# Self attention: where TensorE weighs a batch within a step

## What is computed

```python
def _L1_attn_ref(x, Wqkv, Wout, Wpos, coeffs):
    ...
    pos_bias = jnp.einsum('ijf,hf->hij', pos_feat, Wpos)
    qkv = jnp.einsum('bsd,ed->bse', x, Wqkv)
    q, k, v = jnp.split(qkv, 3, axis=-1)
    ...
    logits = jnp.einsum('bihd,bjhd->bhij', q, k) * scale + pos_bias[None]
    attn = jax.nn.softmax(logits, axis=-1)
    out = jnp.einsum('bhij,bjhd->bihd', attn, v).reshape(B, S, D)
    return jnp.einsum('bsd,ed->bse', out, Wout)
...
    x = x + _L1_attn_ref(_layernorm(x, axis=-1), L1_attn_Wqkv, L1_attn_Wout, L1_attn_Wpos, L1_attn_coeffs)
```

## Time and profile before

| | |
|---|---|
| time, three runs | 1470.67, 1470.76, 1476.12 us; median 1470.76 |
| span of the profiled execution | 1470.8 us; the page gives no other time for it |
| busy, TensorE / VectorE / ScalarE / GpSimd | 94% / 62% / 54% / 45% of the span |
| mean granted clock of TensorE | 0.984 of full speed |
| the stage of the change | about 714 to 956 us |

### The profile page before, as it was taken

How to read it: one execution, slowest core, us unless ns; L and a number is a source line. 1 busy time by engine, 2 the same in 40 slices (tenths; PEclk the granted TensorE clock), 3 DMA queues, 4 the chain that set the end, 5 groups by cost and what they waited for, 6 DMA issues and landing times.

```text
span 1470.8 us, 38209 instructions
## 1 busy us (share of the span) xinstructions
PE 1379.5 (94%) x14581; PEld 1051.8 (72%) x14581; DVE 917.2 (62%) x2370; ACT 796.8 (54%) x1526; POOL 655.2 (45%) x680
## 2 busy tenths in 40 slices
PE   6999999997999989999789998899999999998997
PEld 5667667666777777887556666678888888885864
DVE  3344444436889975435789988785677767766123
ACT  4544545444788864545467675655545455542521
POOL 3344445334326642006777776543334444443034
PEclk9999999999999999999899999999999999999999
DMA  5020330000475812237000000000000000001323
GB/s 164 20 66 23 89 118 8 12 1 6 178 281 210 288 51 82 80 122 276 23 10 2 2 2 2 2 14 6 7 2 11 12 12 8 9 11 50 111 59 90
DMA packets 97820, 92.60 MB, mean 63 GB/s; under 512 B 21869, under 2 KB 71658, under 8 KB 97386
## 3 DMA queue, kind: packets, MB, share of 16 engines
q1 hardware_dynamic: 93034, 80.71, 16.9%
q0 software_dynamic: 4608, 9.45, 2.1%
HBM read 31.92 MB, written 58.21 MB: 61 GB/s over the span
## 4 chain that ended last, share of the span: by engine, by line
PE 77%; DVE 9%; ACT 6%; issue 4%; POOL 3%; DMA 1%; SPq 1%; DVEq 0%; ACTq 0%; POOLq 0%
PE bank L3238 6%; PE bank L1641 5%; PE bank L1625 5%; PE bank L3273 5%; PE bank L3252 4%; PE bank L3226 4%; PE bank L947 4%; PE bank L874 4%; PE bank L880 4%; PE bank L903 3%; PE bank L924 3%; PE bank L2611 3%; PE bank L2621 3%; PE bank L3264 2%; PE bank L891 2%
## 5 line engine op out<-in xcount | busy, mean ns | idle before, releaser
L1407 ACT COPY s_pT<-bank 77x512 f32<-77x512 f32 (+1 forms) x256 | 134.7, 584 | 70.0 <-PE bank L1625 69.9
L3010 POOL TENSOR_TENSOR s_p<-s_p,s_inverse 128x616 f32<-128x616 f32 x64 | 76.9, 1221 | 202.1 <-DVE s_inverse L3153 202.1
L1625 PE MATMUL bank<-ident,s_p 128*77 128x128 f32 (+1 forms) x1024 | 140.4, 284 | 18.9 <-ACT s_p L1398 18.5
L1625 PEld LDWEIGHTS bank<-ident,s_p 128*77 128x77 f32 (+1 forms) x1024 | 116.3, 148 | 46.8 <-ACT s_p L1398 30.5
L1294 POOL TENSOR_TENSOR s_p<-s_p,s_peak 128x1024 f32<-128x1024 f32 x64 | 120.1, 1897 | 39.8 <-DVE s_peak L1493 39.8
L1398 ACT ACTIVATE s_p<-s_p 128x616 f32<-128x616 f32 (+1 forms) x128 | 110.7, 888 | 26.2 <-POOL s_p L1294 22.5
L3137 DVE TENSOR_REDUCE s_peak<-bank 128x8 f32<-128x616 f32 x64 | 50.8, 793 | 93.7 <-PE bank L3252 93.7
L753 DVE TENSOR_TENSOR s_aT<-bank,s_weight 128x512 f32<-128x512 f32 (+1 forms) x64 | 44.1, 690 | 96.9 <-PE bank L924 58.1
L3238 PE MATMUL bank<-pos_bias,s_ctx 128*32 128x128 f32 x3072 | 90.5, 274 | 1.7 <-ACT s_kT L3048 1.7
L3068 ACT ACTIVATE s_p<-s_p 128x616 f32<-128x616 f32 x64 | 46.8, 731 | 81.8 <-DVE s_p L3141 81.8
L1479 DVE TENSOR_TENSOR s_p<-bank,pos_bias 128x1024 f32<-128x1024 f32 x64 | 77.6, 1216 | 18.2 <-PE bank L1614 18.2
(11 more groups left out here) (366 smaller groups left out, 3380.9 us busy)
## 6 DMA issues: line engine op xcount, KB each, us to landing
sorted_tokens<-s_zero SPq DMA_DIRECT2D x4, 5632.0 KB
sorted_tokens<-s_zero SPq DMA_DIRECT2D x8, 2560.0 KB, 13.2
routed_tokens<-s_routed SPq DMA_DIRECT2D x24, 256.0 KB, 2.3
s_tokens<-sorted_tokens SPq DMA_DIRECT2D x48, 64.0 KB, 1.9
s_rows<-sorted_tokens SPq DMA_DIRECT2D x48, 64.0 KB, 1.9
x_all<-x SPq DMA_DIRECT2D x8, 256.0 KB, 3.0
w_s_gateup<-s_gateup SPq DMA_DIRECT2D x1, 2048.0 KB
out<-x_all SPq DMA_DIRECT2D x8, 256.0 KB, 2.9
```

What stands on the lines that cost most here:

```text
L1407: nc.scalar.copy(pT[0:keys, b % 2, 4 * q:4 * q + 4, :].rearrange("m h t -> m (h t)"), bank[0:keys, flip_bank("p", b, q), :]).then_inc(drai ...
L1625: last = nc.tensor.transpose(bank[0:keys, into, j * T:(j + 1) * T], p[:, b % 2, 4 * q + j, :], core.ident[:, :])
L3010: nc.gpsimd.tensor_tensor(part, part, inverse[:, b % 2, heads].unsqueeze(2).to_broadcast([P, HU, M]), ALU.mult).then_inc(share_ready, 1)
```

## The change

`weigh` moves within TensorE's step, for the self attention alone: from between the two halves of the transposes to behind the transposes of the normalised x, next to the scores. All other engines' programs stay as they are.

```diff
                 flip_p(step - 1, 0)
             if not cross and step % G == 3 and g < GROUPS:
                 project_k(g)
-            if not cross and 2 <= step < BATCH + 2:
-                weigh(step - 2)
             if step % G == 3 and g < GROUPS:
                 project_q(g)
             if step % G == 1 and step < BATCH:
...
                 flip_p(step - 1, 1)
             if step % G == 2 and g < GROUPS:
                 flip_xn(g)
+            if not cross and 2 <= step < BATCH + 2:
+                weigh(step - 2)
             if not cross and step + 1 < BATCH:
                 scores_of(step + 1)
```

## The result

The changed kernel takes 1493.94 us (median of 4 runs, 1492.21 to 1496.02); the kernel before took 1472.26 (4 runs, 1470.67 to 1476.12). The ratio is 1.0146, 95% interval [1.0127, 1.0164]: 21.7 us slower. The forecast was 1502, range 1487 to 1514. It stood on the first three runs of the kernel before, median 1470.76; a fourth moved the median to 1472.26. A span is 1.7 to 1.9 us less than the time of the same execution wherever both are on record (1490.5 and 1492.31 here), so the span of 1470.8 belongs to an execution of about 1472.6 us.

The account below looks back on a forecast made before the run. TensorE (25.17 us busy) and VectorE (24.98) were taken to bound the group of 27.37 us. Start 1470.8, plus 23 for order (17.8, 2.35, 1.3, 1.6), plus 8 for the clock, gave 1502 us, range 1487 to 1514.

Parts of the forecast that it names:

- value step: Step with the values' projection: ScalarE's copy of the values waits for the weighing, starting at 5.3 us, not 4.10; +1.2 us.
- norm step: Step with the norm's transposes: second half waits for its exponential, then weighing, reciprocal, product, output follow; 7.1 against 6.23, +0.9 us.
- key step: Step with two projections, both exponentials ready: halves, projections, weighing, reciprocal, product, output in a row; 7.75 against 7.50, +0.25 us.
- plain step: Step without extra TensorE work: VectorE's product lies only 0.95 us ahead, so its chain reaches 7.4 into the step; +1.2 us.
- five groups, batches 4 to 23: Five full groups of four batches, each 3.55 us longer by the four steps' sum; 17.8 us together.
- batches 24 to 31: Last two groups: 2.35 us for batches 24 to 27, without norm work behind the key step, and 1.3 for the last.
- end of the stage: The two last weighings no longer lie beside a second half; weighing 30 starts behind both halves; about 1.6 us.
- clock: TensorE's new waits in the norm step's approach: one fall to 1.2 GHz in most groups, six at 1.3 us, +8; chance 0.55.
- no clock fall: Rival for the whole kernel: order alone costs 23 us and the clock stays, 1494 us; chance 0.27.
- The slack of 0.84 us: Rival at VectorE's reciprocal: weighing may come 0.84 us later unmissed, leaving 0.14 a step, 4.5 us, 1475; chance 0.05.
- Faster: Rival on ScalarE: earlier second-half copies and exponentials remove TensorE's idle 2.20 us a group, 15 us, 1455; chance 0.03.

Follow-up runs that it names:

- The first run that removed the exponential's wait: Changed kernel with ScalarE's second exponential of the norm step ahead of the last two activations of the norm: 1493.70 us, ratio 1.0150.
- the second, with both out of the way: Changed kernel; in the norm step second exponential and first half's copies ahead of the last two activations, weighing ahead of the normalised x's transposes: 1494.74 us, ratio 1.0153.
- the key step alone: Kernel before with the weighing moved only in steps with step % 4 = 3: 1476.48 us, ratio 1.0029.
- the value step alone: Kernel before with the weighing moved only in steps with step % 4 = 1: 1486.67 us, ratio 1.0095.
- the plain step alone: Kernel before with the weighing moved only in steps with step % 4 = 0: 1473.35 us, ratio 1.0004.
- the moments first: Changed kernel with VectorE's moments of the norm ahead of the reciprocal and product in the key step: 1494.59 us, ratio 1.0162.
- the two kernels that had them: Kernel before, weighing moved in value step only, plus ten transposes: 1482.97 us; changed kernel, moments ahead of the reciprocal except in the last key step, plus ten: 1486.12.

## Why the prediction was right, and where its terms were off

The direction and the mechanism of the order held: waits that the weighing covered came out, and what depends on it came late. The forecast of the time was 8 us too high, and what I held most likely, one fall of the clock in most groups, did not come. The profiled execution grew by 19.7 us; its steps add up to that, and the terms compare so:

| term | forecast | measured | where |
|---|---|---|---|
| value step | +1.2 | +1.40 | 8.84 |
| norm step | +0.9 | +0.71 | 6.94 |
| key step | +0.25 | -0.26 | 7.24 |
| plain step | +1.2 | +1.35 | 7.55 |
| five groups, batches 4 to 23 | 17.8 | 13.8 | 4 x 3.2 and 0.95 |
| batches 24 to 31 | 3.65 | 3.9 | up to the last first half: 46.22 before, 50.15 after |
| end of the stage | 1.6 | 1.9 | last first half to the next stage's matmuls: 9.57 before, 11.47 after |
| clock | +8 | +1.3 in the profiled execution, inside the rows above | norm steps of 7.54 and 7.65; no fall from 752 to 889 |

*Value step.* Right in mechanism, shown by two runs: moved there alone it makes 8.84, and with the copy of the values out of the way it is 7.11. The second half's wait for its bank was 0.43 us where I had 0.3, and from the weighing to the copy it is 2.10 us (792.00 to 794.10), not 2.0.

*Norm step.* The predicted wait for the exponential was there, 0.62 us. What I did not see is that the bank of the second half's last four transposes comes free at nearly the same time. In the changed kernel the copy that frees it starts at 798.98 and takes about 0.59 us, so it ends at 799.57, and those transposes follow at about 799.6. The first run that removed the exponential's wait met the bank instead; the second, with both out of the way, made 6.18. The normalised x is not a third condition of the changed kernel, as I had written ahead of that run: its activations end at 798.13 there, 2.0 us ahead of its transposes at 800.10. It would be one only where ScalarE takes these activations last: they end at 771.91 in that kernel, and TensorE weighs from 771.30. The output to the next transposes, 0.60 from the earlier trace rows, is 0.33 where the output itself starts after a wait, as in nearly all steps now. Where it follows the scores at once it stays near 0.6 (774.84 to 775.47 in the run that made 6.18); why is not settled.

*Key step.* The wrong sign comes from the same 0.60, and from the first half and the two projections: 0.87, 0.86 and 0.86 us in a row, where I counted 0.92 and 2 x 0.96 from rows between weighings. The product is late all the same, and that is what the plain step pays.

*Plain step.* Shown by the key step alone (7.56 with the plain step's weighing at its old place) and by the moments ahead of the product (6.33). The product lies 0.67 us ahead of the step (810.94 to 811.61), not 0.95, and the chain from it to the next step takes 8.2 us (810.94 to 819.16), not 8.35: two errors that partly cancel.

*The sum over groups.* The step that failed is "five full groups: 17.8". Four grew by 3.2 us each. The fifth, with VectorE's late results, grew by 0.95: the kernel before stood still there for 3.54 us ahead of a weighing and had the clock at half level after it (11.80 us for the step, mean clock 0.71), and in the changed kernel the second half stood ahead of that wait (2.67 us, 10.28 for the step). This is a gain of the move that I had not counted. The changed kernel's clock fell in this step too (mean 0.83), at no price that shows: the same step without a fall is 10.27 (905.33 to 915.60, in the kernel with norm steps of 6.18).

*The clock.* Mis-sized. I expected one fall in most groups; in the profiled execution the steady part had none:

```profile
752.00:889.00 137.00, 110.06 (x1677) 79.39 (x1676) 111.13 (x162) 86.13 (x140) 94.41 (x76) 1.00 0.01 2
```

Falls came in two later norm steps, 7.54 and 7.65, and each cost 0.6 to 0.7 us where I had 1.3: the clock was low from the step's start, and the wait of 0.62 us ahead of the second half was gone in these steps. In the three other executions of the changed kernel (mean clock 0.980, 0.983 and 0.987; spans 1494.2, 1493.8 and 1490.4) the two with the lower clock are 3.5 us longer. The mean over its four executions is 0.9835, over 60 executions of the kernel before 0.986, and among those 60 a clock lower by 0.001 goes with about 0.6 us more. From these comparisons I put the clock's term at 1 to 4 us, an estimate; the executions without a trace do not show where their clock fell. The place was mostly right: of the falls in the changed kernels' steady parts most came in the norm step, behind the output between two waits, but the kernel with the copy of the values last fell in two value steps and in no norm step.

That the median, 1493.94, is the number of the rival "no clock fall", 1494, is in part luck. The rival's sum had the order 3 us too high (23, where the whole of the profiled execution grew by 19.7), no clock, and a start 1.5 us too low, and these nearly cancel.

The Trainium skill, "TensorE: Matmul & The Clock Gate", section "A second HAM failure mode: psum-queue depth-cycling", says that frequent short pauses between groups of matmuls can make the clock go to and fro between its levels. The traces agree in part: with the value step alone four of six norm steps fell (7.75 to 7.86 us), in the changed kernel two of six (7.54 and 7.65), with the same wait of 1.58 us ahead of all of them.

*The other rivals.* The slack of 0.84 us did not absorb the move, since the second half did wait for bank and exponential. Faster is excluded. In the plain step alone the move is free (1.0004): there the weighing ends by 811.05 (809.99 and 1.06 of its last row), and VectorE comes to the reciprocal at 811.11 without a wait for it. The slack is real where nothing else moves.

## What to carry to other kernels

Before a long instruction group is moved on one engine, list what the other engines have queued behind the instruction that waits for it: here one copy on ScalarE, 0.6 us long, carried about half of the price, and putting it last took that back. Where a wait is removed and nothing changes, look at the row behind it: another condition may end at nearly the same time, and both must go. When matmuls are placed so that waits gather on both sides of a short one, look at the granted clock of that place in several executions, not in one.

## What the runs showed that I had not expected

- What a fall of the clock in the norm step costs depends on where the step's own wait stands to it. With no wait left in the step it is 1.5 to 1.6 us (7.86 for 6.23, value step alone; 7.72 for 6.18). With the wait of 0.62 us behind the fall, the fall uses the wait up and costs 0.6 to 0.7 us (7.54 for 6.94). With the same wait ahead of the fall, it costs 1.55 (8.49 for 6.94): there the first half and the wait passed at full clock. The four falls with the moments first lie between, 0.85 to 1.27. The norm step of 8.49 with two stretches of it, and behind the dots that of 7.54 with its first part:

```profile
851.78:860.27 8.49, 7.51 (x95) 5.83 (x96) 5.08 (x7) 6.39 (x10) 3.93 (x3) 0.80 0.01 3
851.78:853.41 1.63, 1.09 (x8) 0.85 (x8) 1.63 (x3) 1.63 (x4) 0.18 (x1) 1.00 0.02 5
853.50:856.50 3.00, 3.00 (x22) 2.63 (x26) 1.73 (x2) 2.40 (x5) 2.32 (x2) 0.54 0.03 5
...
889.17:896.71 7.54, 7.20 (x94) 5.87 (x95) 4.22 (x6) 6.18 (x10) 3.75 (x2) 0.79 0.01 2
889.17:892.00 2.83, 2.83 (x13) 2.69 (x14) 2.59 (x3) 2.62 (x5) 1.28 (x1) 0.50 0.00 0
```

- The same waits do not always bring a fall. With 1.58 us ahead of the norm step's first half and 0.62 behind it, four norm steps in a row kept the full clock in the changed kernel, and four in a row did not with the moments first. What decides between them is open; each kernel was profiled once.
- With ten transposes that nobody reads, 1.26 us of TensorE in a wait of 1.58, no norm step fell in either of the two kernels that had them, twelve steps in all.
